# A selective scan and an attention layer on one core: products with C in pairs, norms and gates without scalar forms on VectorE

## The reference

```
xn = layernorm(x)
x  = x + mamba_ffn(xn) + experts(xn)       # layer 0
xn = layernorm(x)
x  = x + attention_memory(xn) + mlp(xn)    # layer 1

# the scan in mamba_ffn, for each of 512 channels and 16 states n
h_t = exp(delta_t * A) * h_{t-1} + delta_t * B_t * u_t
y_t = sum over n of h_t * C_t,   y = (y + u * D) * silu(res)
# behind it, per sequence: c = m + ffn(m);  (c - mean(c)) / sqrt(var(c) + 1e-5)

# in attention_memory, per token and head
gated = mean over heads of sigmoid(mem_score * mem_scale) * sigmoid(x @ memg_w + memg_b)
out   = (seq_out + gated * (x @ memv_w + memv_b)) @ out_w + out_b
```

## Time and profile before

| | us |
|---|---|
| median of 3 runs | 3743.68 (3743.35 to 3746.09) |
| the profiled execution, its own time | 3741.8 |
| its span, first to last instruction | 3740.1 |
| busy: PE, DVE, ACT, POOL | 3550.8, 3189.5, 2646.2, 2274.0 |
| mean granted TensorE clock | 0.986 of full |

### The profile page before, as it was taken

One profiled execution on the slowest core, in us unless ns is written; L12 is line 12 of the kernel. 1 busy time (PEld: TensorE's weight loads), 2 busy tenths in 40 slices (PEclk: granted clock), 3 DMA queues, 4 the chain that ended last, 5 costly groups with the idle time before them and its releaser, 6 DMA issues.

```text
span 3740.1 us, 63542 instructions
## 1 busy us (share of the span) xinstructions
PE 3550.8 (95%) x20512; PEld 2365.2 (63%) x20512; DVE 3189.5 (85%) x6108; ACT 2646.2 (71%) x4045; POOL 2274.0 (61%) x1788
## 2 busy tenths in 40 slices
PE   7999999999999999999887999999999999999998
PEld 3666666656656665666664766667666666766665
DVE  3888999999999999999977788796978879697873
ACT  6868888788787888888634757666675756667565
POOL 3788999999999999999934142332414233241421
PEclk9999999999999999999997999999999999999999
DMA  4445455455554555555622123232312323231230
GB/s 154 150 155 162 162 162 172 153 170 167 168 163 155 174 168 168 162 168 162 199 91 94 39 82 96 70 113 67 117 45 79 100 70 112 67 117 45 78 90 21
DMA packets 253340, 456.88 MB, mean 122 GB/s; under 512 B 26116, under 2 KB 80852, under 8 KB 250196
## 3 DMA queue, kind: packets, MB, share of 16 engines
q1 hardware_dynamic: 253012, 452.82, 39.1%
HBM read 381.07 MB, written 69.21 MB: 120 GB/s over the span
## 4 chain that ended last, share of the span: by engine, by line
PE 47%; DVE 22%; issue 10%; ACT 6%; POOL 6%; DMA 2%; DVEq 0%; SPq 0%; POOLq 0%; ACTq 0%
DVE ps L2064 7%; PE ps L1659 6%; PE ps L1546 5%; PE ps L1651 5%; PE ps L1527 4%; PE ps L1509 4%; DVE heavy L2042 3%; POOL drive L2321 3%; PE ps L1411 3%; PE ps L1461 2%; DVE held L2064 2%; DVE ps L2087 2%; PE ps L1586 2%; PE ps L1378 2%; ACT ps L1676 2%
## 5 line engine op out<-in xcount | busy, mean ns | idle before, releaser
L2321 POOL TENSOR_TENSOR drive<-du,b_wide 128x1024 f32<-128x1024 f32 x512 | 1202.9, 2367 | 138.1 <-DVE ps L2064 66.6
L1676 ACT ACTIVATE ps<-delta,neg_a 128x512 f32<-128x512 f32 x1024 | 683.3, 685 | 166.4 <-DVE heavy L2042 132.3
L1676 ACT ACTIVATE exps<-ps 128x1024 f32<-128x1024 f32 (+1 forms) x640 | 599.3, 938 | 280.3 <-PE ps L1527 275.3
L2355 POOL TENSOR_SCALAR_AFFINE_SELECT exps<-exps 128x256 f32<-128x256 f32 x512 | 202.5, 410 | 976.6 <-ACT exps L1676 976.6
L2087 DVE CUSTOM_DVE_ANT_0 ps<-ps,later 128x512 f32<-128x512 f32 (+3 forms) x1024 | 474.8, 516 | 84.7 <-PE ps L1509 83.7
L1461 PEld LDWEIGHTS ps<-p_all,heavy 128*128 128x128 f32 x3072 | 358.0, 143 | 168.8 <-issue 80.8
L2042 DVE TENSOR_TENSOR heavy<-c_wide,ps 128x512 f32<-128x512 f32 x704 | 448.5, 669 | 11.3 <-issue 10.4
L1461 PE MATMUL ps<-p_all,heavy 128*128 128x128 f32 x3072 | 419.0, 277 | 35.8 <-DVE heavy L2042 27.6
L2064 DVE TENSOR_TENSOR_SCAN ps<-ps,carry,drive 128x512 f32<-128x512 f32 x352 | 435.4, 1271 | 4.1 <-ACT ps L1676 3.8
L2064 DVE TENSOR_TENSOR_SCAN ps<-ps,drive 128x512 f32<-128x512 f32 x352 | 412.8, 1209 | 19.6 <-ACT ps L1676 15.6
L2307 POOL TENSOR_TENSOR held<-held,c_wide 128x1024 f32<-128x1024 f32 x160 | 378.5, 2366 | 6.4
(11 more groups left out here) (211 smaller groups left out, 7174.6 us busy)
## 6 DMA issues: line engine op xcount, KB each, us to landing
c_wide<-bc_dram SPq DMA_DIRECT2D x512, 256.0 KB, 3.6
b_wide<-bc_dram SPq DMA_DIRECT2D x512, 256.0 KB, 3.4
stacks<-parts SPq DMA_DIRECT2D x192, 256.0 KB, 2.5
qs<-stacks SPq DMA_DIRECT2D x128, 192.0 KB
ks<-stacks SPq DMA_DIRECT2D x128, 192.0 KB, 4.3
x_row<-in_x SPq DMA_DIRECT2D x14, 1024.0 KB, 7.9
resid<-mix SPq DMA_DIRECT2D x9, 1024.0 KB, 5.4
x_row<-resid SPq DMA_DIRECT2D x9, 1024.0 KB, 5.4
```

The source lines that it names most:

```text
L1676: return nc.scalar.activation(out_, in_, func, **kw)
L2321: G.tensor_tensor(drive[:, g % DRIVE_SLOTS, :, :], du[:, e, :, :], wide(b_wide[:, g % B_SLOTS, :], MD), ALU.mult).then_inc(driven, 1)
```

## The change

Four things change together.

- **Products with C by pairs.** A weigh now takes both steps of a group in one instruction of 128x1024: it reads the two neighbouring PSUM banks and C twice (a broadcast view), and writes two pieces of the ring. It waits for the second scan. The semaphore `weighed` counts groups, so PE's add of the first piece, ACT's decay into either bank and SP's load of the next C all wait for the pair.
- **The gate of layer 0** is one instruction of 128x4x256 in place of four.
- **Norms.** `guard` is gone: epsilon is the bias of ACT's square root, in both layers. The factor -1 is no longer in `offset` and `shift`: ACT writes the negated means to `ln_minus`, and DVE negates the mean of the sequence as it empties the bank. `offset` and `shift` are TENSOR_TENSOR with two operands in SBUF in place of SCALAR_TENSOR_TENSOR with two operands in SBUF. `square` becomes two TENSOR_TENSORs (a product, then a sum), with a wait between them.
- **The gates of layer 1.** ACT adds the ones (and the factor 16 of the mean) in two more instructions; DVE keeps a product, the reciprocal, the sum over heads, and one product of 128x1024 for the four tiles of z.

The lengths that the planner uses for these tasks, and the searched constants, are new, so the order changes all over the program. Of the table of constants two lines are shown.

```diff
+def weighed_before(g):
+
+    pairs, n = g // NS, g % NS
+    return pairs * (NS - len(POOL_STATES)) + n - sum(m < n for m in POOL_STATES)
...
-                if not by_pool(n):
-                    full_ring = piece - d + 1 - W_SLOTS
-                    add("v", ("weigh", k), 0.59, k + 1.5, ("v", "scan", k), ("s", "c", g),
-                        only(full_ring >= 0, ("p", "add", full_ring)))
-                    add("p", ("add", piece), 0.44, k + LEAD0["add"], ("v", "weigh", k))
-        add("v", ("gate", q), 1.32, at + NS * MD + 0.7, ("p", "add", piece_of(j, e + 1, 0, 0) - 1),
+            if not by_pool(n):
+                piece = piece_of(j, e, n + 1, 0)
+                full_ring = piece + 1 - W_SLOTS
+                add("v", ("weigh", g), 1.13, MD * g + 2.5, ("v", "scan", MD * g + MD - 1), ("s", "c", g),
+                    only(full_ring >= 0, ("p", "add", full_ring)))
+                for d in range(MD):
+                    add("p", ("add", piece + d), 0.44, MD * g + d + LEAD0["add"], ("v", "weigh", g))
...
-            add("v", ("guard", b), 0.3, at + NT, ("v", "spreads", b), ("a", "norm", b - 1, NT - 1))
-            add("a", ("root", b), 2.7, at + NT, ("v", "guard", b))
+            add("a", ("root", b), 2.9, at + NT, ("v", "spreads", b), ("a", "norm", b - 1, NT - 1))
...
-            add("a", ("logistic", b, c), 0.5, place["ms", b, c, 1], ("v", "ms", b, c, 1))
-            add("v", ("gate", b, c), 3.2, place["ms", b, c, 1], ("a", "logistic", b, c), ("v", "pb", b, TC * c + TC - 1))
+            add("a", ("logistic", b, c), 0.95, place["ms", b, c, 1], ("v", "ms", b, c, 1))
+            add("v", ("gate", b, c), 2.1, place["ms", b, c, 1], ("a", "logistic", b, c), ("v", "pb", b, TC * c + TC - 1))
...
-SHORT, RUN, STAY = 0, 2, 0.02
-PULL = {"a": 0.026, "v": 0, "g": 0.009, "s": 0.0}
+SHORT, RUN, STAY = 0, 1, 0.02
+PULL = {"a": 0.026, "v": 0, "g": 0.002, "s": 0.0}
...
-    ("v", 0): {"scan": 45, "weigh": -77, "guard": 31},
+    ("v", 0): {"scan": 49, "weigh": -47},
...
-                    sp.wait_ge(weighed, weighs_to(MD * (old + 1)))
+                    sp.wait_ge(weighed, weighed_before(old) + 1)
...
-                        pe.wait_ge(weighed, weighs_to((q * NS + states[u - 1]) * MD) + d + 1)
+                        pe.wait_ge(weighed, weighed_before(q * NS + states[u - 1]) + 1)
...
-                    act.wait_ge(guard_done, parts_done(j, task[-1]))
-                    f(ln_rstd[:, part], ln_rstd[:, part], ACT.Sqrt).then_inc(root_done, 1)
+                    act.wait_ge(spread_done, parts_done(j, task[-1]))
+                    act.wait_ge(norm_done, NT * j)
+                    f(ln_minus[:, part], ln_mv[:, part, 0], ACT.Copy, scale=-1.0).then_inc(minus_done, 1)
+                    f(ln_rstd[:, part], ln_mv[:, part, 1], ACT.Sqrt, bias=eps).then_inc(root_done, 1)
...
-                        act.wait_ge(weighed, weighs_to(old) + 1)
+                        act.wait_ge(weighed, weighed_before(old // MD) + 1)
...
-                    f(ln1_rstd[:, :], ln1_rstd[:, :], ACT.Sqrt).then_inc(ln_sqrt, 1)
+                    act.wait_ge(xn_done, NT * n)
+                    f(ln1_rstd[:, :], ln1_mv[:, :, 1], ACT.Sqrt, bias=eps).then_inc(ln_sqrt, 1)
...
-                    f(mem_in[:, TC * c:TC * (c + 1), :], mem_in[:, TC * c:TC * (c + 1), :], ACT.Exp, scale=-1.0)
-                    f(gate_in[:, TC * c:TC * (c + 1), :], gate_in[:, TC * c:TC * (c + 1), :], ACT.Exp, scale=-1.0)\
-                        .then_inc(sig_done, 1)
+                    own = slice(TC * c, TC * (c + 1))
+                    f(mem_in[:, own, :], mem_in[:, own, :], ACT.Exp, scale=-1.0).then_inc(ones_added, 1)
+                    f(gate_in[:, own, :], gate_in[:, own, :], ACT.Exp, scale=-1.0).then_inc(ones_added, 1)
+                    act.wait_ge(ones_added, 2 * (NC * n + c) + 1)
+                    f(mem_in[:, own, :], mem_in[:, own, :], ACT.Identity, bias=heads, scale=heads).then_inc(sig_done, 1)
+                    act.wait_ge(ones_added, 2 * (NC * n + c) + 2)
+                    f(gate_in[:, own, :], gate_in[:, own, :], ACT.Copy, bias=1.0).then_inc(sig_done, 1)
...
-                elif kind == "guard":
-                    dve.wait_ge(spread_done, parts_done(b, part))
-                    dve.wait_ge(norm_done, NT * b)
-                    V.tensor_scalar(ln_rstd[:, tiles_of(b, part)], ln_mv[:, tiles_of(b, part), 1], EPS, None, ALU.add).then_inc(guard_done, 1)
...
-                    V.scalar_tensor_tensor(ln_shift[:, own], ln_mv[:, own, 0], -1.0, ln_rstd[:, own], ALU.mult, ALU.mult)\
-                        .then_inc(offset_done, 1)
+                    dve.wait_ge(minus_done, parts_done(b, part))
+                    V.tensor_tensor(ln_shift[:, own], ln_minus[:, own], ln_rstd[:, own], ALU.mult).then_inc(offset_done, 1)
...
-                    V.tensor_copy(row_q[:, 0:1], bank[:, 0:1]).then_inc(drained_v, 1)
+                    V.tensor_scalar(row_q[:, 0:1], bank[:, 0:1], -1.0, None, ALU.mult).then_inc(drained_v, 1)
                 elif kind == "square":
-                    dve.wait_ge(row_apart, b + 1)
-                    V.scalar_tensor_tensor(row_q[:, 1:2], row_q[:, 4:5], row_q[:, 4:5], row_mv[:, 1:2], ALU.mult,
-                                           ALU.add).then_inc(row_square, 1)
+                    dve.wait_ge(row_apart, 2 * b + 1)
+                    V.tensor_tensor(row_q[:, 5:6], row_q[:, 4:5], row_q[:, 4:5], ALU.mult).then_inc(row_apart, 1)
+                    dve.wait_ge(row_apart, 2 * b + 2)
+                    V.tensor_tensor(row_q[:, 1:2], row_q[:, 5:6], row_mv[:, 1:2], ALU.add).then_inc(row_square, 1)
...
-                    V.scalar_tensor_tensor(row_q[:, 2:3], row_q[:, 0:1], -1.0, row_q[:, 3:4], ALU.mult, ALU.mult)\
-                        .then_inc(row_shift, 1)
+                    drained(dve, L0_PLAN, ("mu", b), "v")
+                    V.tensor_tensor(row_q[:, 2:3], row_q[:, 0:1], row_q[:, 3:4], ALU.mult).then_inc(row_shift, 1)
...
-            def weigh(k):
-                j, e, n, d = k // STEPS, k // (NS * MD) % ND, k // MD % NS, k % MD
-                g, piece = k // MD, piece_of(j, e, n + 1, d)
-                dve.wait_ge(scanned, k + 1)
-                if d == 0 and piece + 1 >= W_SLOTS:
+            def weigh(g):
+                j, e, n = g // GROUPS, g // NS % ND, g % NS
+                piece, bank = piece_of(j, e, n + 1, 0), DECAY_BANKS[MD * g % len(DECAY_BANKS)]
+                dve.wait_ge(scanned, MD * (g + 1))
+                if piece + 1 >= W_SLOTS:
                     dve.wait_ge(piece_added, piece - W_SLOTS + 2)
-                if d == 0:
-                    dve.wait_ge(c_in[g % C_SLOTS], 16 * (g // C_SLOTS + 1))
-                V.tensor_tensor(heavy[:, piece % W_SLOTS, :], c_wide[:, g % C_SLOTS, :], state_bank(k),
+                dve.wait_ge(c_in[g % C_SLOTS], 16 * (g // C_SLOTS + 1))
+                first = piece % W_SLOTS
+                V.tensor_tensor(heavy[:, first:first + MD, :], wide(c_wide[:, g % C_SLOTS, :], MD), ps[:, bank:bank + MD, :],
                                 ALU.mult).then_inc(weighed, 1)
 
             def gate_pair(j, e):
                 dve.wait_ge(piece_added, piece_of(j, e + 1, 0, 0))
                 dve.wait_ge(held_added, len(POOL_STATES) * (j * ND + e + 1))
                 dve.wait_ge(gate_silu, j + 1)
-                for t in range(TC):
-                    part = of_pair(gate[j % 2][:, t, :], e)
-                    V.tensor_tensor(part, acc_tile(t), part, ALU.mult).then_inc(y_gated, 1)
+                part = gate[j % 2][:, :, e * MD * P:(e + 1) * MD * P]
+                V.tensor_tensor(part, ps[:, 0:2, :].rearrange("p b (h d) -> p (b h) d", h=2), part, ALU.mult)\
+                    .then_inc(y_gated, TC)
...
-                    link("v", last)
-                    V.tensor_scalar(ln1_rstd[:, :], ln1_mv[:, :, 1], EPS, None, ALU.add).then_inc(ln_var, 1)
+                    last.then_inc(ln_var, 1)
...
-                    dve.wait_ge(sig_done, NC * b + c + 1)
-                    link("v", V.tensor_scalar(mem_in[:, tiles, :], mem_in[:, tiles, :], 1.0, None, ALU.add))
-                    link("v", V.scalar_tensor_tensor(mem_in[:, tiles, :], gate_in[:, tiles, :], 1.0, mem_in[:, tiles, :],
-                                                     ALU.add, ALU.mult))
+                    dve.wait_ge(sig_done, 2 * (NC * b + c + 1))
+                    link("v", V.tensor_tensor(mem_in[:, tiles, :], gate_in[:, tiles, :], mem_in[:, tiles, :], ALU.mult))
                     link("v", V.reciprocal(mem_in[:, tiles, :], mem_in[:, tiles, :]))
                     link("v", V.tensor_reduce(gate8[:, tiles], mem_in[:, tiles, :], AX_X, ALU.add))
-                    link("v", V.tensor_scalar(gate8[:, tiles], gate8[:, tiles], 1.0 / H, None, ALU.mult))
-                    for t in range(TC * c, TC * (c + 1)):
-                        last = V.tensor_scalar(z[b % 2][:, t, :], z[b % 2][:, t, :], gate8[:, t:t + 1], None, ALU.mult)
```

(4 more changed lines are left out.)

38 lines of the change are left out of this document (21 added, 17 removed), and 15 rows, old and new, of the table SHIFTS.

## The result

| | us |
|---|---|
| median before, in the runs beside it | 3744.15 (3743.35 to 3746.09, 4 runs) |
| median of the changed kernel | 3767.42 (3760.34 to 3770.09, 4 runs) |
| ratio | 1.0059, interval 1.0047 to 1.0072 |
| the profiled execution of the changed kernel, its span | 3760.3, 3758.6 |
| busy: PE, DVE, ACT, POOL | 3548.0, 3150.2, 2651.1, 2279.2 |

I forecast 3731 us, 13 faster. The kernel became 23 us slower, outside my range (3700 to 3757). DVE has 39 us less work over the launch, as forecast or more; the time went the other way.

What follows compares the result with a forecast made beforehand. The prediction took DVE to bound layer 0 (500 to 1800 us) and PE layer 1. Layer 0 -6, transition -2 and layer 1 -5 made -13 from the median 3743.7, so 3731 us, range 3700 to 3757.

Steps and rivals of the forecast that it cites:

- The pair's product, -25 us: Layer 0, DVE: one product over two banks takes 1.11 us, saving 0.07 us for each of 352 pairs, -25 us.
- Dependent weighs, +8: Layer 0, DVE: 70 more weighs directly behind the scan they wait for, at 0.11 us each, +8 us.
- The gate of layer 0, -7: Layer 0, DVE: four gate instructions become one, 0.23 us less at each of 32 gates, -7 us.
- The norms: Layer 0, DVE: two-SBUF-operand products still wait for POOL; guard -7.8 us, offset and shift 0, square +16.
- the scalar form was the cause: Rival, layer 0's norms: plain products would not wait for POOL, so -33 us there, 3702 us in all; chance 0.18.
- DVE's busy time in the stretch, -10: Layer 0, 500 to 1800 us: DVE's busy time over the same number of scans should fall by 10 us.
- The added wait, +5: Layer 0: banks freed in pairs delay DVE's scans by 0.4 us at each of 12 ACT gelus, +5 us.
- The rival of starved scans: Layer 0: scans run short of banks behind all 56 long ACT functions, +39 us, 3765 us in all; chance 0.17.
- The transition, -2: Between the layers, 1800 to 2100 us: layer 1's first statistics move among the last scans, -2 us.
- Layer 1, -5: Layer 1: changed gates save DVE 17 us, of which 5 count since PE is the limit; new order uncharged.
- DVE's gain is taken by the others: Rival: POOL's and PE's chains already set layer 0's pace and layer 1 stays PE's, 3743 us; chance 0.20.
- A microsecond taken from DVE is worth one: Layer 0, some 400 to 1890 us: DVE savings shorten the run one for one until PE or POOL fills.

Runs made afterwards that it cites:

- b_acts: Kernel before with layer 1's changed gates, and layer 0's norms without DVE instructions that wait for POOL (small ACT instructions instead): 3721.9 us, ratio 0.9947.
- Experiment 3: Kernel before, each with one condition changed: first bank released only after both weighs of a pair, 3857.6 us; first piece likewise, 3827.6 us.
- b_lateadd: Kernel before, with PE's add of a pair's first piece waiting until both pieces are there: 3827.6 us, ratio 1.0217.
- experiment 4: Kernel before with only layer 1's changed gates, 3730.8 us; changed kernel with layer 1's old order, 3737.1; three small reorderings of the changed kernel, 3759.4 to 3770.5.
- experiment 5: Kernel before plus layer 1's changed gates, then layer 0 lightened: norms off DVE 3721.9 us, that plus merged gate 3717.5, narrower weighs 3715.0, narrower POOL drive 3718.8.

## Why the prediction was wrong, step by step

Two steps of it failed. The added wait in layer 0 was charged with 5 us and ate the whole gain there. The new order of layer 1 was a term put at nothing, for want of a sign, and cost 27 to 30 us. Term by term:

- **The pair's product, -25 us.** Right: 1.12 us from start to start against 1.11 taken, -21 for 352.
- **Dependent weighs, +8.** Right: 0.12 us at each, 68 more than before, +8.
- **The gate of layer 0, -7.** Right: 44.8 us busy became 38.7; alone, on top of b_acts, it brought gate 31 5 us earlier.
- **The norms.** The mechanism was right: two operands in SBUF wait for POOL whatever the form (1314, 1207 and 2006 ns), so the rival "the scalar form was the cause" (3702) fell. `guard` went, and `offset` and `shift` together changed by -1 (12.6 + 7.3 to 9.2 + 9.7). `square` is off in size: +8.7 us, not +16 (10.3 to 16.0 + 3.0). Both products wait for POOL, and the second in full (2.27 us), as charged. But I let the first wait as long as the old instruction (1.29 us on average); it comes near the end of POOL's drive and took 0.375. That is its place in the order, which I had not worked out.
- **DVE's busy time in the stretch, -10.** It fell by 16, mostly because `square` cost less than charged.
- **The added wait, +5. This step failed.** I charged it at ACT's gelus alone, and behind them the waits did grow by 4.2 us. But DVE's waits for ACT grew by 9.5 in all (10.7 to 20.2; I had read only the 8.0 of the scans in place), with 8.4 us behind ACT's `mix`, where there had been none, and those for POOL and DMAs, for which I charged nothing, by 8.5. Experiment 3 gives the late release of banks and of pieces alone, at the old places: +111 and +81 us, no small charge beside a gain. That the new order brings this back and pays for it with the gain of 16 is my reading: shown are 155 us more in the old order and some 0 in the new one, not what the order trades for it. I had PE's late add at 0, on the ground that PE has 64 us of room. But room over a stretch says nothing on a wait in a ring: in b_lateadd PE has the same work, and waits 84 us for pieces instead of 13. Layer 0 came to 0 instead of -6 in the stretch, and to +6 to +10 with all up to layer 1 by the medians and the ratios (experiment 4), where -8 was forecast. The rival of starved scans named the right mechanism, with 39 us at four functions per half sequence; the waits that it prices at 39 grew by 9.5 in the changed kernel. (It counts 56 of them in the stretch, the trace has 47: 33 us.)
- **The transition, -2.** From gate 26 to the first bias mark: 403.9 us before, 406.3 after, +2: inside the bounds of -8 and +8, on the other side of zero.
- **Layer 1, -5. This step failed too, and is the larger one.** The gates alone gave -14, at the edge of the bounds (0 and -15). The new order gave +27 to +30: PE waits some 16 us longer from 2100 to 3700, and runs 27 us of it at half clock. I wrote that it "may move this stage by as much again; I have no sign for it", and charged nothing. With the whole DVE order of layer 1 in view, and PE with 42 us of idle time in 1600, any other order could hardly gain more than those 42 and could lose far more. That skew belonged in the range and in the chances.
- **The rival "DVE's gain is taken by the others".** For the stretch in layer 0 its outcome is what came: 1003 us from gate 8 to gate 26 in both, within 0.04 us, with POOL's and PE's busy times within 4 us. That both differences are so near to nothing is luck, since the order was new. Its reason, chains of POOL and PE that set the pace, holds in part: experiment 5 gets 0.3 to 0.8 for a microsecond of DVE.
- **"A microsecond taken from DVE is worth one".** It fell: 0.3 to 0.8 in experiment 5, in the order of before.

What stays open: which of the moves in the new order of layer 1 makes its exponentials and maxima late. The order as a whole is shown to cost that much; the two places tested are not the cause. The 48 us that the new order costs the old instructions lie in layer 1 too (sequences of 225 us, gate 31 at 1895.4). One wait of PE of 3.5 us stands in each of its sequences, with 6.8 us of half clock; what it waits for was not looked into.

## What to carry to other kernels

Merging two instructions into one also merges their signals. Before counting the saved microseconds, list who waits for the first half, and how deep their buffers are: here, with a ring of four banks and one of six pieces, the merged instructions cost 155 us in the old order, against 21 saved by the merged product. When a change brings new instructions and a new order, judge them apart by crossing them; here the new gates were worth -14 and the order of that layer +27 to +30, and the best kernel kept the old order, the early releases and only the local savings. A wait that shows at the end of a chain of late things is not yet their cause: remove it and see whether the next one takes its place.

## What the runs showed of the hardware

- A DVE instruction on one column with both operands in SBUF, beside POOL, lasts until POOL's instruction in flight is over: 2.27 us at 744.94, ending within 0.01 us of POOL's. How long it lasts is set by when it comes: the one before it, at 744.55, took 0.36. With no POOL instruction in flight both took 0.15 (at 1985.3). The same kind of arithmetic on ACT, one column at a time, took 0.28 us each in b_acts (64 copies with a scale; they overlap, 12.7 us busy in all).
- A product over two PSUM banks costs 1.12 us from start to start, two over one bank 1.18, so 0.06 us for the instruction saved, next to nothing against a late release. A dependence on the instruction directly before costs 0.12 us. The Trainium skill (VectorE: DVE Perf Modes, "Rules for kernel authors") makes the number of DVE instructions the thing to cut. The trace agrees in the sign and shows how little it is here.
- TensorE's granted clock fell to 1.2 GHz for 3.4 or 6.8 us once in each of six sequences of layer 1 in the changed kernel, with a wait of PE of 0.7 to 1.3 us beside its start. The length of that wait alone does not decide: five waits of 1.38 us in the same trace (2734.7 for one) are followed by no low stretch, and of seven waits of 1.66 us in the kernel before only two are (2240.7 and 3113.9). How it is decided, the runs do not show.
